# Token shift of a norm's input by a transfer, a new order of the groups, and a rebuilt cross-attention stage

## The chip, the core and the metric

The kernel runs on one core of one Trainium2 chip. The metric is the device time of one execution in microseconds (us), median of the runs. The engines are named as in the profile: PE (TensorE matmul) and PEld (its weight loads), DVE (VectorE), ACT (ScalarE), POOL (GpSimd) and SP (SyncE, which here only issues transfers). All data are float32.

## What is computed

x has 32 batches of 128 tokens with 128 features. First comes a cross-attention with 16 query heads of 8 features and 4 key/value heads, then six layers, each of a local attention (16 heads of 64, windows of 32 tokens that also see the window before) and a gated feed-forward part:

```
x = x + xattn(layernorm(x), ctx, ctx, deltas, mask, Wq, Wk, Wv, Wo, tw)
  # scores = q k^T / sqrt(8) + tw * log1p(|ct_i - ct_j|) + (1 - mask) * -1e9;  ct = cumsum(deltas)
z = layernorm(x)
for i in range(6):
    z = attn_layer(shift_tokens(z), Wqkv[i], q_scale[i], k_scale[i], Wo[i]) + z
    z = ffn_layer(shift_tokens(z), ln_g[i], ln_b[i], W1[i], b1[i], W2[i], b2[i]) + z
return x + z
# shift_tokens: features 64 to 127 come from the token before (zero for token 0), 0 to 63 stay
# attn_layer: q, k divided by their norms, scaled, rotated; softmax over 64 keys; @ Wo
# ffn_layer: layernorm of its input, @ W1 + b1, a * gelu(gate), @ W2 + b2
```

## The kernel before

Tokens lie on the 128 partitions. z_sb holds z of all batches ([128, 32 x 128]), x1_sb the sum after the cross-attention. There is one program for each engine, written out by hand. Engines meet only through semaphores: `count(per_unit, unit, j)` is the value a semaphore has after step j of a unit, `wait` waits for it. Each engine takes its instructions in order, so a wait holds back all that stands behind it on that engine.

**First stage** (`xslots` / `xslot`, lines 252 to 259, 398, 502, 729, 1019). 35 slots; slot n works on batch A = n, Bt = n - 1, C = n - 2 and D = n - 3. For A: PE transposes ctx and the normed x (lines 1051, 1052), and `ones @ td` (line 1053) gives the cumulated deltas and the mask on all rows; DVE makes mbr, dif and dabs (779 to 783) from these, ACT the logarithm (530) and DVE the bias (801); PE projects q, k and v (1078 to 1080), ACT writes qT (534), DVE kblk (813) and vaug (825). For Bt: four score products of 512 columns on a group of 32 rows each (1030), DVE adds the bias (742) and takes maxima (752), POOL subtracts them (409), ACT takes the exponential (545). For C: 16 transposes of 128 x 128 (1071), ACT copies (523), and P times v (1094), copied by ACT (539). For D: four transposes (1042), division by the row sums (760, 770), a transpose (1060), the product with Wo, called y (1086), and on DVE x1cur = y + x (793), its statistics, a copy to x1_sb (806) and the norm into z_sb (829). `rows` (713) makes on DVE the normed x and both halves of td for the batch after A.

**Second stage** (`slots` / `slot`, lines 237 to 244, 418, 549, 834, 1103). A unit is one batch in one layer: 192 units, one new unit in each slot, some 199 slots. In slot n the engines work on a = n (q, k, v), m = n - 1 (inverse norms, `root`), b = n - 2 (transposes, scores, softmax), c = n - 3 (P times v, `attend`), d = n - 4 (attention's output `attn_out`, second shift and norm, gate) and f = n - 5 (`ffn_out`). The order within a slot is the list of calls at the end of each `slot` function (lines 973 to 994 on DVE, 1279 to 1297 on PE, 653 to 674 on ACT, 476 to 488 on POOL).

Around the second shift: `attn_out` (1225; 16 matmuls, line 1233) writes y to bank 7; DVE's `z_mid` (891) adds z: zm. PE's `shift_tokens` (1237) multiplies the first half of zm by the identity (1242) and the second by a shift matrix (1243) into bank 6. DVE takes statistics from there (`norm_stats` 898, `norm_aggr` 905, `norm_var` 911), POOL the power -1/2 (450), DVE applies them (`norm_apply` 918), PE transposes (1258), ACT scales (620), and the gate and a products follow (1267, 1275). POOL's `residual` (459) adds b2 to the unshifted zm for `z_out` (882) in the next slot.

The q and k products (`proj_qk(j)`, line 1123) use banks 0 and 1 by turns: each waits until `rotary` (852, 855; d_rot) and `square` (563) have read what was there before; `proj_v` (1133) waits for the last two rotaries.

**SP** issues all transfers in one queue, in order. The second stage's own are `shift_v(u)`: six transfers of 64 rows of 2 KB from vt to vs, within SBUF, after ACT has copied v and after PE has done `attend` of unit u - 2. In all there are 1,308 transfers: 1,152 of shift_v; in each layer 17 (wqkv in two pieces, rot, wo, gb 2, b1c 6, w1, w2 3, b2r); and 54 at the start and the end (constants 1, dm 2, x 4, Wq, Wk, Wv, Wo and the time weight 5, q and k scales 2, ctx 32, out 8). gb and b1c are columns of 4-byte rows, FCH cuts 341 features into 128, 128 and 85, so two of the six b1c transfers and one of the three w2 transfers have 85 rows, the others 128. Wk and Wv have 128 rows of 128 bytes, the time weight 128 rows of 4 bytes. At a change of layer SP waits in order for the last use of each weight (`load_qk` 278, `load_v`, `load_o`, `load_ffn` 297, which waits for p_y2, that is `ffn_out` of the layer's last unit).

## Time and profile before

| | |
|---|---|
| median of 3 runs | 3447.68 us (3443.36 to 3448.49) |
| the profiled execution | 3448.77 us, its span 3446.8 us, mean granted PE clock 0.976 |
| busy: PE / PEld | 3301.8 us (96%) / 2378.3 us (69%) |
| busy: DVE / ACT / POOL | 2931.5 (85%) / 2735.7 (79%) / 2502.3 us (73%) |
| the chain that ended last | PE 76%, POOL 9%, issue 7%, DVE 4%, DMA 1% |

### The profile page before, as it was taken

Reading aid. Unit: us, or ns where it says so; the run is one execution under the profiler, and the core shown is the slowest. Engines: PE = TensorE matmul, PEld = TensorE weight load, DVE = VectorE, ACT = ScalarE, POOL = GpSimd, SP = SyncE. Lnnn points to the kernel's source line nnn. Section 1 sums busy time; section 2 is a strip of 40 time slices with the busy share of each in tenths; the row PEclk is TensorE's granted clock in tenths of the full one; section 3 lists DMA queues with packets and bytes.
Section 4 is the critical chain, followed back from the end, with each engine's and each line's share of the span. In section 5 each row is a group of like instructions: output and inputs, shape, how many; then the busy total and the mean of one; then the engine's idle time right before and its main releaser. Section 6 shows DMA issues by size and latency. Waiting matters only on the chain.

```text
span 3446.8 us, 169053 instructions
## 1 busy us (share of the span) xinstructions
PE 3301.8 (96%) x65316; PEld 2378.3 (69%) x65316; DVE 2931.5 (85%) x6259; ACT 2735.7 (79%) x5169; POOL 2502.3 (73%) x2671
## 2 busy tenths in 40 slices
PE   5888789999999999999999999999999999999997
PEld 3444357777777777777777777777777777777775
DVE  6888788888888888888888888888888888888885
ACT  3445588888888888888888888888888888888886
POOL 3333377777778777777778777777778777777774
PEclk9778899999999999999999999999999999999998
DMA  2000021212221211222122211212221112212122
GB/s 75 5 6 5 2 55 49 55 46 55 65 68 46 54 51 49 81 53 55 46 55 62 71 50 50 55 46 75 59 55 47 53 52 68 67 46 55 46 55 54
DMA packets 125539, 175.91 MB, mean 51 GB/s; under 512 B 26742, under 2 KB 49332, under 8 KB 124724
## 3 DMA queue, kind: packets, MB, share of 16 engines
q1 hardware_dynamic: 125492, 175.28, 18.9%
q8 instruction: 30, 0.49, 0.1%
q14 instruction: 17, 0.14, 0.0%
HBM read 21.32 MB, written 2.10 MB: 7 GB/s over the span
## 4 chain that ended last, share of the span: by engine, by line
PE 76%; POOL 9%; issue 7%; DVE 4%; DMA 1%; SPq 1%; ACT 1%; POOLq 0%; DVEq 0%; ACTq 0%
PE bank L1123 16%; PE bank L1233 9%; PE bank L1141 9%; PE bank L1133 8%; PE bank L1204 7%; PE bank L1188 6%; POOL qk L435 4%; POOL qk L444 4%; PE bank L1267 3%; PE bank L1221 3%; PE bank L1275 3%; PE bank L1030 2%; PE bank L1071 2%; PE bank L1242 2%; PE bank L1180 2%
## 5 line engine op out<-in xcount | busy, mean ns | idle before, releaser
L435 POOL TENSOR_TENSOR qk<-ta,tb 128x512 f32<-128x512 f32 x768 | 982.8, 1280 | 11.6 <-DVE tb L855 11.6
L1123 PE MATMUL bank<-wqkv,zsT 128*128 128x512 f32 x1536 | 806.4, 607 | 6.1 <-DVE tb L855 2.4
L444 POOL TENSOR_TENSOR qk<-qk,rn 128x512 f32<-128x512 f32 x768 | 796.0, 1049 | 0.0
L563 ACT ACTIVATE sq<-bank 128x512 f32<-128x512 f32 x768 | 461.0, 600 | 322.9 <-PE bank L1123 313.5
L473 POOL TENSOR_TENSOR P<-P,rowsum 128x512 f32<-128x512 f32 x384 | 401.4, 1046 | 374.7 <-DVE rowsum L971 374.7
L852 DVE TENSOR_TENSOR ta<-bank,rot 128x512 f32<-128x512 f32 x768 | 525.8, 685 | 25.4 <-ACT sq L563 10.0
L855 DVE TENSOR_TENSOR tb<-bank,rot 128x512 f32<-128x512 f32 x768 | 521.2, 679 | 0.0
L956 DVE TENSOR_REDUCE bank<-sq 128x32 f32<-128x2048 f32 x192 | 437.8, 2280 | 0.3
L1133 PE MATMUL bank<-wqkv,zsT 128*128 128x512 f32 x768 | 412.3, 619 | 5.0 <-DVE tb L855 5.0
L1233 PE MATMUL bank<-wo,oT 128*128 128x128 f32 x3072 | 393.9, 281 | 1.4 <-ACT oT L589 1.4
L1233 PEld LDWEIGHTS bank<-wo,oT 128*128 128x128 f32 x3072 | 357.4, 191 | 14.6 <-ACT oT L589 1.8
L1141 PEld LDWEIGHTS bank<-cst,qk 64*128 64x128 f32 x6144 | 222.1, 139 | 173.2 <-issue 150.4
L1123 PEld LDWEIGHTS bank<-wqkv,zsT 128*128 128x128 f32 x1536 | 257.1, 198 | 105.1 <-issue 96.5
L1204 PE MATMUL bank<-PT,vs 64*64 64x32 f32 (+1 forms) x18432 | 307.9, 220 | 1.1 <-issue 0.7
L1204 PEld LDWEIGHTS bank<-PT,vs 64*64 64x64 f32 x18432 | 286.5, 135 | 31.7 <-issue 31.7
L450 POOL TENSOR_TENSOR rstd<-ve,half_neg 128x1 f32<-128x1 f32 x192 | 105.7, 550 | 264.4 <-DVE ve L911 264.4
L1188 PEld LDWEIGHTS bank<-kT,qT 64*32 64x32 f32 x24576 | 277.4, 105 | 15.6 <-issue 5.4
L1188 PE MATMUL bank<-kT,qT 64*32 64x64 f32 x24576 | 281.0, 225 | 4.7 <-issue 4.7
L891 DVE TENSOR_TENSOR zm<-bank,z_sb 128x128 f32<-128x128 f32 x192 | 55.9, 291 | 265.1 <-PE bank L1233 265.1
L409 POOL TENSOR_TENSOR qk<-qk,xmax 128x512 f32<-128x512 f32 x128 | 130.0, 1047 | 205.0 <-DVE xmax L752 205.0
L1141 PE MATMUL bank<-cst,qk 64*128 64x64 f32 x6144 | 274.4, 229 | 3.7 <-issue 1.9
L573 ACT ACTIVATE qT<-bank 128x512 f32<-128x512 f32 x384 | 229.1, 597 | 47.8 <-PE bank L1141 47.7
(132 smaller groups left out, 6528.8 us busy)
## 6 DMA issues: line engine op xcount, KB each, us to landing
vs<-vt SPq DMA_DIRECT2D x1152, 128.0 KB, 2.4
wqkv<-L_ffn_Wqkv SPq DMA_DIRECT2D x6, 1024.0 KB, 5.1
wqkv<-L_ffn_Wqkv SPq DMA_DIRECT2D x6, 512.0 KB, 3.8
wo<-L_ffn_Wo SPq DMA_DIRECT2D x6, 512.0 KB, 3.7
z_sb<-x SPq DMA_DIRECT2D x4, 512.0 KB, 6.7
ctxb<-ctx SPq DMA_DIRECT2D x32, 64.0 KB, 1.8
out<-x_sb SPq DMA_DIRECT2D x8, 256.0 KB, 3.5
w<-L_ffn_W SPq DMA_DIRECT2D x6, 341.0 KB, 3.1
```

The source lines that it names most:

```text
L435: g.tensor_tensor(o, i0, i1, ALU.add).then_inc(s["g_add"], 1)
L444: g.tensor_tensor(q3, q3, r3, ALU.mult).then_inc(s["g_qk"], 1)
L563: a_.activation(sq[:, 512 * j:512 * j + 512], bank[j % 2][:, :], ACT.Square)\
L852: v_.tensor_tensor(ta[:, c].rearrange("p (h d) -> p h d", d=DH), bank[j % 2][:, :].rearrange("p (h d) -> p h d", d=DH), rot[:, o:o + 64].u ...
L855: v_.tensor_tensor(tb[:, c].rearrange("p (h c d) -> p h c d", c=2, d=32)[:, :, ::-1, :], bank[j % 2][:, :].rearrange("p (h c d) -> p h c d ...
L956: v_.tensor_reduce(sm, sq[:, :].rearrange("p (h d) -> p h d", d=DH), AX.X, ALU.add)\
L1123: t_.matmul(bank[j % 2][:, :], zsT[:, k % 2, :], wqkv[:, 512 * j:512 * j + 512], start=True, stop=True).then_inc(s["p_qk"], 1)
L1133: t_.matmul(bank[r][:, :], zsT[:, k % 2, :], wv[:, :, r, :], start=True, stop=True)\
L1141: ins = t_.transpose(bank[4 + t][:, 64 * p:64 * p + 64], src[tok, 128 * p:128 * p + 128], ident[tok, tok])
L1188: ins = t_.matmul(SC[e][32 * w:32 * w + 32, 64 * p:64 * p + 64], qT2[dr, p, 32 * w:32 * w + 32], kT2[dr, p, k0:k0 + 64], start=False, stop ...
L1204: ins = t_.matmul(bank[4 + r][64 * e:64 * e + 64, 128 * i + q0:128 * i + q0 + nq], vs[kr, pc, w, hc:hc + 64], PT[kr, 4 * e + i, q0:q0 + nq ...
L1233: ins = t_.matmul(bank[7][:, 384:512], oT[:, p, :], wo[:, 2 * (p % 4) + p // 4, :], start=p == 0, stop=p == PAIRS - 1)
```

## The change

1. **Second shift.** `shift_tokens` on PE goes. zm gets three parts of 64 columns: `z_mid` writes parts 0 and 2, and SP sends part 2 of rows 0 to 126 to part 1 of rows 1 to 127 (`shift_z`); row 0 of part 1 is zeroed once. DVE's statistics and `norm_apply` read parts 0 and 1 from SBUF, after waiting for the transfer (l_s0, l_s1). The other reader, `residual`, takes parts 0 and 2.
2. **Order of the second stage's calls**, on all four engines. `attend` now waits itself for vs.
3. **SP's queue**: `shift_z(u)` stands ahead of `shift_v(u + 3)`, and among the loads at a change of layer.
4. **Root.** The rotary constants are multiplied by 2^8, the logarithm's input and the constant -0.5 by 2^16.
5. **First stage.** td, mbr and dif go: dcur (two columns, copied by POOL) is the stationary operand against tri and ident, ACT takes the absolute value with -ct as bias, and the bias is added from PSUM. The normed x moves from DVE to ACT (`center`, with nmr0 = -mean * rstd), the copy to x1_sb too. P is transposed in 32 pieces of 64 rows. The orders of all four engines change.

```diff
-        zm = sb("zm", [128, 2, E])
+        zm = sb("zm", [128, 2, 3, E // 2])
@@ SP
+            def shift_z(u, par):
+
+                wait(sp, "d_zm", count(1, u, 1))
+                sp.dma_start(zm[1:128, par, 1, :], zm[0:127, par, 2, :]).then_inc(s[f"l_s{par}"], 16)
...
                     for k in range(2):
+                        shift_z(i * 2 + (start + k), k)
                         shift_v(i * 2 + (start + 3 + k), (3 + k) % 2)
+                shift_z(end - 6, 0)
                 shift_v(end - 3, 1)
+                shift_z(end - 5, 1)
                 if layer + 1 < DEPTH:
                     load_qk(layer + 1)
                 shift_v(end - 2, 0)
                 if layer + 1 < DEPTH:
                     load_v(layer + 1)
+                shift_z(end - 4, 0)
                 shift_v(end - 1, 1)
+                shift_z(end - 3, 1)
                 if layer + 1 < DEPTH:
                     shift_v(end, 0)
+                shift_z(end - 2, 0)
+                if layer + 1 < DEPTH:
                     shift_v(end + 1, 1)
                     load_o(layer + 1)
+                shift_z(end - 1, 1)
+                if layer + 1 < DEPTH:
                     shift_v(end + 2, 0)
                     load_ffn(layer + 1)
@@ DVE, second stage
-                        v_.tensor_tensor(zm[:, pd, :], bank[7][:, 384:512], z_sb[:, cols(d)], ALU.add)\
+                        v_.tensor_tensor(zm[:, pd, 0:3:2, :], bank[7][:, 384:512].rearrange("p (c e) -> p c e", c=2),
+                                         z_sb[:, cols(d)].rearrange("p (c e) -> p c e", c=2), ALU.add)\
...
-                        wait(dve, "p_zsh", count(1, d, 1))
-                        v_.bn_stats(stats[:, 0:6], bank[6][:, 0:128]).then_inc(s["d_bn"], 1)
+                        wait(dve, f"l_s{pd}", 16 * (d // 2) + 16 if isinstance(d, int) else (d >> 1) * 16 + 16)
+                        v_.bn_stats(stats[:, 0:6], zm[:, pd, 0:2, :].rearrange("p c e -> p (c e)"))\
+                            .then_inc(s["d_bn"], 1)
@@ PE, first stage
-                    t_.matmul(bank[6][:, 256:512], ones[:, :], td[:, pA, :], start=True, stop=True)\
-                        .then_inc(s["x_A1"], 1)
+                    t_.matmul(bank[6][:, 256:384], dcur[:, pA, 0:1].to_broadcast([128, S]), tri, start=True, stop=True)
+                    t_.matmul(bank[6][:, 384:512], dcur[:, pA, 1:2].to_broadcast([128, S]), ident,
+                              start=True, stop=True).then_inc(s["x_A1"], 1)
```

The orders of the second stage, after (before, they are as printed in the functions above):

```
PE:   proj_qk(0) transpose_qk(0) attn_out proj_qk(1) transpose_qk(1) transpose_z ffn_out proj_qk(2)
      transpose_P scores attend transpose_zn proj_qk(3) proj_v(0) ffn_gate ffn_a proj_v(1)
DVE:  z_mid root(0) rotary(0) root(1) root(2) root(3) norm_stats norm_aggr norm_var z_out rotary(1)
      norm_apply maximum(0) rotary(2) maximum(1) subtract(0) rotary(3) subtract(1) sum_squares gated
      sum_rows invert
ACT:  copy_T(0) copy_T(1) square(0) log_sum square(1) inverse_root copy_T(2) copy_T(3) copy_z
      copy_PT(0) copy_PT(1) square(2) [table] copy_o(0) copy_zn square(3) copy_v(0) copy_o(1) gelu
      [table] exponent copy_v(1)
POOL: norm_rstd add(0) add(1) next_input normalize(0) residual normalize(1) normalize(2) normalize(3)
      add(2) add(3) weigh(0) weigh(1)
```

The orders of the first stage, after:

```
PE:   xscores(0) xscores(1) transpose_P(0) [D: O transposed] xscores(2) [A: ctx, xn, deltas] xscores(3)
      transpose_P(1) [D: attn transposed] [A: q, k, v] [D: y] [C: P times v]
DVE:  add_bias(0) add_bias(1) [D: 1/sums] maximum(0) [D: attn] add_bias(2) add_bias(3) maximum(1)
      [D: x1cur] [A: kblk] [D: statistics, variance] [A: bias, vaug] [D: norm into z_sb]
ACT:  copy_P(0) [A: abs, cxT] copy_P(1) [D: attnT] center(A + 1) [A: qT] exponent(0) [D: x1_sb]
      [A: logarithm] [C: copy of O] exponent(1)
POOL: subtract(0,0) subtract(0,1) subtract(1,0) [D: power] subtract(1,1) deltas_of(A + 1)
```

## Rows read from the trace of the kernel before

**Rows 1.** Busy time by stretch: start:end, length, engines, granted clock, DMA share, GB/s.

```profile
100.00:200.00 100.00, 81.27 (x416) 47.80 (x415) 83.29 (x219) 48.73 (x93) 37.56 (x41) 0.81 0.02 6
...
2000.00:2500.00 500.00, 498.90 (x10735) 368.12 (x10734) 436.47 (x904) 424.75 (x807) 394.06 (x421) 1.00 0.21 56
```

**Rows 2.** Busy time in one slot of the second stage (columns as in rows 1).

```profile
1602.69:1618.13 15.44, 15.44 (x335) 11.38 (x332) 13.44 (x28) 13.14 (x25) 12.20 (x13) 1.00 0.19 51
```

**Rows 3.** Timeline of PE, one slot of the second stage: start, length, what.

```profile
1602.69 2.05 PE L1233 MATMUL bank<-wo,oT 128*128 128x128 f32 x16
...
1606.17 0.43 PE L1242 MATMUL bank<-zm,cst 128*128 128x64 f32 x2
...
1606.67 1.10 PE L1123 MATMUL bank<-wqkv,zsT 128*128 128x512 f32 x2
...
1618.13 2.05 PE L1233 MATMUL bank<-wo,oT 128*128 128x128 f32 x16
```

**Rows 4.** Timeline of DVE in the same slot; in brackets the idle time before.

```profile
1604.97 0.29 DVE L891 TENSOR_TENSOR zm<-bank,z_sb 128x128 f32<-128x128 f32 x1 [1.67 <-PE bank L1233]
...
1606.87 0.30 DVE L898 BATCH_NORM_STATS2 stats<-bank 128x6 f32<-128x128 f32 x1 [0.17 <-PE bank L1243]
...
1619.00 0.29 DVE L882 TENSOR_TENSOR z_sb<-bank,zmb 128x128 f32 x1 [0.56 <-issue]
...
1620.41 0.29 DVE L891 TENSOR_TENSOR zm<-bank,z_sb 128x128 f32<-128x128 f32 x1 [1.02 <-PE bank L1233]
```

**Rows 5.** Transfers: the page's part 6, then line 285 by itself.

```profile
vs<-vt SPq DMA_DIRECT2D x1152, 128.0 KB, 2.4
...
ctxb<-ctx SPq DMA_DIRECT2D x32, 64.0 KB, 1.8
...
L285 SPq DMA_DIRECT2D rot<-rot_all x6: 484/496/553, 18.5 to 2884.6; - x6
...
DMA to landing us min/median/max: 2.1/3.2/3.3
```

**Rows 6.** The page, part 2: packets of all transfers by size.

```profile
DMA packets 125539, 175.91 MB, mean 51 GB/s; under 512 B 26742, under 2 KB 49332, under 8 KB 124724
```

**Rows 7.** DMA of 953 to 960 us (GB/s in 40 slices), then of 100 to 300 us.

```profile
GB/s 211 129 0 0 0 0 0 0 79 193 170 301 316 295 345 342 342 339 199 67 6 0 0 0 0 0 0 0 0 0 0 0 0 0 0 0 0 0 0 0
...
q1 hardware_dynamic: 2448, 1.12, 1.9%
```

**Rows 8.** First stage: line 1030 in all, then two of its slots on PE.

```profile
L1030 PE MATMUL bank<-kblk,qT x256: 587/692/1218, 27.3 to 399.5; 32*128 32x512 f32 x128
...
216.74 1.23 PE L1030 MATMUL bank<-kblk,qT 32*128 32x512 f32 x4 [1.13 <-DVE kblk L813]
...
227.60 2.19 PE L1030 MATMUL bank<-kblk,qT 32*128 32x512 f32 x4 [2.84 <-DVE kblk L813]
```

**Rows 9.** Timeline of DVE at the end of the first of those slots.

```profile
224.20 0.28 DVE L793 TENSOR_TENSOR x1cur<-bank,z_sb 128x128 f32<-128x128 f32 x1
...
224.73 0.97 DVE L801 SCALAR_TENSOR_TENSOR bias<-lnt,xtwc,mbr 128x128 f32<-128x128 f32 x1
225.62 1.06 DVE L806 COPY x_sb<-x1cur 128x128 f32 x1
...
226.69 0.65 DVE L813 TENSOR_TENSOR kblk<-bank,cst 128x512 f32<-128x512 f32 x1
```

**Rows 10.** Busy time by stretch around those slots (columns as in rows 1).

```profile
216.70:224.76 8.06, 7.67 (x49) 4.52 (x49) 7.64 (x22) 4.66 (x10) 2.79 (x4) 1.00 0.03 8
224.76:227.60 2.84, 0.00 (x1) 0.01 (x1) 2.84 (x8) 2.51 (x3) 1.96 (x3) 0.97 0.00 0
227.60:238.80 11.20, 11.20 (x41) 6.97 (x42) 7.22 (x19) 3.36 (x9) 3.24 (x4) 0.55 0.02 6
```

**Rows 11.** The chain of waits at one change of layer: start, length, what.

```profile
897.21 5.21 DMA wqkv<-L_ffn_Wqkv
...
972.82 3.28 DMA b2r<-L_ffn_b
```

More of the change, by code:

```diff
@@ L40 @@
 NORM_MIN2 = 1e-24
+LN_UP = 2.0 ** 16
 MASKED = -(2.0 ** 120)
@@ L398, in xslot @@
             def xslot(n, k):
+                A1, A1_on = part(n, -1, B)
                 Bt, B_on = part(n, 1, B)
@@ L499, in _, with center @@
             act.wait_ge(s["u_ct"], 1)
-            a_.activation(ctT[:, :], bank[6][:, 64:96], ACT.Copy).then_inc(s["u_ctc"], 1)
+            a_.activation(nct[:, :], bank[6][:, 64:96], ACT.Copy, scale=-1.0).then_inc(s["u_ctc"], 1)
+            def center(A, pA):
+                wait(act, "x_A1", count(1, A - 2, 1, B))
+                if isinstance(A, int) and A <= 4:
+                    act.wait_ge(s["u_nmr"], 1 if A < 4 else 2)
+                a_.activation(xn[:, pA, :], z_sb[:, bass.ds(A * E, E)], ACT.Identity, scale=rstd0[:, bass.ds(A, 1)],
+                              bias=nmr0[:, bass.ds(A, 1)]).then_inc(s["x_xn"], 1)
+            act.wait_ge(s["l_x"], 64)
+            center(0, 0)
             def xslot(n, k):
+                A1, A1_on = part(n, -1, B)
                 A, A_on = part(n, 0, B)
@@ L517, in xslot @@
                     a_.activation(attnT[:, :], bank[7][:, 0:128], ACT.Copy).then_inc(s["x_aTc"], 1)
[L518 to L525 removed]
+                if A1_on:
+                    center(A1, (k + 1) % 2)
                 if A_on:
[L528 to L530 removed]
                     wait(act, "x_A2", count(1, A, 1, B))
@@ L534, in xslot @@
                     a_.activation(qT[:, pA, :], bank[6][:, 0:128], ACT.Copy, scale=XSCALE).then_inc(s["x_q"], 1)
+                exponent(0)
+                if D_on:
+                    wait(act, "x_x1", count(1, D, 1, B))
+                    a_.activation(x1_sb[:, bass.ds(D * E, E)], x1cur[:, :], ACT.Copy).then_inc(s["x_store"], 1)
+                if A_on:
+                    wait(act, "x_dabs", count(1, A, 1, B))
+                    wait(act, "x_bias", count(1, A - 1, 1, B))
+                    a_.activation(lnt[:, :], dabs[:, :], ACT.Ln, bias=1.0).then_inc(s["x_ln"], 1)
                 if C_on:
@@ L539, in xslot @@
                     a_.activation(XO, bank[7][:, :], ACT.Copy).then_inc(s["x_Oc"], 1)
-                if B_on:
-                    for j in range(2):
-                        wait(act, "x_sub", count(4, Bt, 2 * j + 2, B))
-                        pr = XP[:, pB, 1024 * j:1024 * j + 1024]
-                        a_.activation(pr, pr, ACT.Exp).then_inc(s["x_exp"], 1)
+                exponent(1)
             xslots(act, xslot)
@@ L1043, in xslot @@
                     ins.then_inc(s["x_OT"], 1)
+                xscores(2)
                 if A_on:
@@ L1284, in slot @@
                 transpose_qk(1)
-                shift_tokens()
+                transpose_z()
+                ffn_out()
                 proj_qk(2)
-                transpose_z()
                 transpose_P()
                 scores()
+                attend()
                 transpose_zn()
                 proj_qk(3)
-                values_here()
                 proj_v(0)
```

309 lines of the change are left out of this document (150 added, 159 removed).

## Prediction

> **What bounds the kernel now.** I read the stretches first: they show two different programs. In the second stage, which holds some 3,000 of the 3,446.8 us, PE is busy 498.9 of 500 us at a full granted clock, DVE 436, ACT 425, POOL 394; in the first nothing is full: PE 81 of 100 us at a granted 0.81, DVE 83, ACT 49, POOL 38 [rows 1]. Busy shares over the whole run hide that. Then I read one slot of each. A slot of stage two runs from 1602.69 to 1618.13 on PE, 15.44 us, and PE is busy for all of them [rows 2, 3]: its instruction stream is the bound. DVE waits 1.67 us in it, in the next one 0.56 and 1.02 [rows 4], so some 13.7 us of its slot is work. Only 1.7 us lie between PE's bound and DVE's own loop, and they are what the change spends. Stage one starts its score products at 27.3 us, and the last of them at 399.5, some 4 us into the 32nd slot [rows 8]: 31 slots in 368 us, 11.9 us each. Its loop closes through DVE: PE has nothing to do from 224.76 to 227.60 and then starts behind kblk (line 813) [rows 8, 10].
>
> **Second stage: removed.** The two shift products (lines 1242, 1243) hold PE from 1606.17 to 1606.67, 0.50 us [rows 3]. Nothing hides them, PE being full. ffn_out, attend and transpose_z move, with their work unchanged; the places where PE's stream breaks ahead of a nop or a wait change, about as many gone as new, which I cost at 0 and round up for: 15.44 - 0.50 = 14.94, call it 15.0 us for PE alone. What the moves put later has room: z_out writes a z_sb that is read 32 units on; ffn_out needs a gated result that DVE has by then; copy_o moves forward on ACT. On POOL, residual goes behind three adds and copies, and its reader z_out belongs to the next slot. The new factor in the square root's logarithm rides on operands that are there: 0.
>
> **Second stage: added.** SP waits for zm, sends 127 rows of 64 values one partition down, and DVE's bn_stats waits for the landing. The wait is in the middle of DVE's queue: behind it stand z_out, three rotaries (PE's v projections and ACT's next squares wait for them), the maxima, subtractions, the sums and at last the next zm. So DVE's own loop counts, in three pieces. (a) From bn_stats to the next z_out is 1619.00 - 0.56 - 1606.87 = 11.57 us of work [rows 4]; two small root steps leave this stretch (-0.3), z_out comes into it (+0.2), and statistics, aggregate and variance follow each other with nothing between (+0.2): 11.7 us to the next zm. (b) zm itself 0.29 [rows 4] and SP's start 0.1: 0.4. (c) the transfer, L. Loop = 12.1 + L. Under L the first rotary and the four root steps (2.0 us) run, which is why L isn't added whole. PE hides the loop up to 15.0, so up to L = 2.9.
>
> **L.** No transfer of this shape is in the trace. The 128 KB ones (64 rows of 2 KB) land in 2.4 us, the 64 KB ones from HBM (128 rows of 512 B) in 1.8, the one within SBUF (128 rows of 1 KB) in 2.1 at its shortest [rows 5]. All these use 16 engines. Does 127 rows? The page counts 26,742 packets under 512 B [rows 6]. Data of that size is 938 rows a layer (gb 256, b1c 512 + 170), 5,628, and 384 at the start (xwk, xwv, xtw): 6,012. The rest, 20,730, is completions. 1,308 transfers (1,152 of vs, 102 of the layers, 54 at the start) with 16 each would be 20,928: 198 are missing. 18 transfers have 85 rows (12 of b1c, 6 of w2), and 18 x 11 = 198. So 85 = 5 x 17 rows went over 5 engines, not 16. 127 has no divisor but 1: one engine takes all 127 packets. The Trainium skill's page "DMA: Bandwidth & Descriptors" (section on why a DMA increments its semaphore by 16) says just this, that the largest number up to 16 that divides the slowest dimension is used, and names 127 partitions as one engine; by it the sum is the forecast, without it the first rival.
> Price of a packet on one engine: 342 GB/s over 16 engines with 512-byte rows is 24 ns a packet, and in the first stage 1.9% of 16 x 200 us over 2,448 packets is 25 ns [rows 7]. Half the bytes is 12 to 13 ns if time goes by bytes, 25 if by packets. 127 packets: 1.6 to 3.2 us. The fixed part is 2.1 less 8 packets of 1 KB, 1.75; from the other rows 1.6 to 2.1. L lies between 3.2 and 5.3; a shorter one than 2.1 [rows 5] isn't to be had. I take 3.35, by bytes, since the rows of 512 B go at a rate set by bytes. The loop is then 12.1 + 3.35 = 15.45 to 15.5 us: the 0.50 us that PE gives up comes back as DVE's wait. 187 steady slots x 0.05: +9 us.
> Not late in either case: POOL with 12.20 and ACT with 13.14 us of work a slot [rows 2], whose queues keep their lengths. SP issues one more transfer a slot; shift_z stands ahead of shift_v, whose wait for attend now ends some 3 us earlier in the slot, so that its six transfers are done when the next zm comes. Without that, shift_z would land behind 128 KB transfers on the same engine. The memset of the row 0 and its wait are at the start: 0.
>
> **Changes of layer.** SP's queue is in order. Now a change of layer costs about 1.3 us (stalls behind the 5.21 us wqkv load and the 3.28 us b2r load [rows 11]). New: the q,k load's stall grows by about 1.5, since attend no longer stands between the last q,k product and the next layer; shift_z(end-1) stands behind the 512 KB of wo (about +2); shift_z of the next layer's first unit stands behind load_ffn, which waits for ffn_out, now later in the slot, and then issues four more (about +3); less what DVE's slack takes. I take 4.5 x 5 = +22 us, bounds 0 and 40. The last three slots, whose chain has nothing beside it: 3 x 1.7 = +5.
>
> **First stage.** DVE loses mbr, dif, dabs (0.8 us with waits), the two td rows and xn, and the copy to x1_sb, which took 1.06 us beside POOL's subtraction as line 801 took 0.97 [rows 9]. After y the way to the next scores was 224.20 to 227.60, 3.4 us: x1 0.28, statistics, bias, copy, aggregate, kblk 0.65 [rows 8, 9]. Now kblk follows x1: 0.3 + 0.65 + 0.25 = 1.2. Saved 2.2 of a slot of 10.86 (216.74 to 227.60). ACT takes on center, Abs and the store, 0.3 each beside 5.8 us of its own (49% of 11.9), which lengthens the copies that y waits for by some 0.3. 32 transposes with 64 rows take PE no longer than 16 with 128; xscores(2) and (3), no longer adjacent, lose their overlap, up to +0.6, partly behind DVE. Slot: 10.86 - 2.2 + 0.3 = 8.9 at the full clock. The clock was granted at 0.55 for the 11.2 us after the idle 2.84 us, and stayed full behind idles near 1.1 [rows 8, 10]. The new idle is about 0.3 to 0.6, so I expect it full, and 31 x (11.9 - 8.9) = -93, and +1 for nmr0 ahead of center at the start: -92. Bounds: +20 (low clock throughout, PE then needs 13 us and more a slot) and -110.
>
> **Sum**, against the profiled execution, 3448.8 (span 3446.8; 1.1 above the median of the runs): 3448.8 + 9 + 22 + 5 - 92 = 3393.
>
> **Rivals.**
> *One: the transfer is cheap* (16 engines, or L under 2.9). For it: 2.1 us in rows 5. Against: the 198 missing completions. PE bounds at 15.0: 187 x -0.44 = -82, changes +10, tail +3, stage one -92: 3288. Chance 0.17.
> *Two: the transfer is dearer by packet* and the kernel slower. Place: bn_stats' wait. Price: each 1 ns of a packet is 0.127 us a slot, 24 us in all. It decides from where it eats what stage one gives, 92 - 27 = 65 us: 0.35 us a slot, a loop of 15.8, L = 3.7, 15 ns a packet. At 20 ns, L = 4.3 and the loop is 16.4: 187 x 0.96 + 27 - 92 = +115, 3563; at 25 ns 3680. For it: half as many bytes needn't halve the time. Against: 512-byte rows stream at the byte rate. Chance 0.28.
> *Three: stage one gives nothing*, since the clock stays low or ACT's longer in-order queue (exponent(1) ahead of copy_P(0)) takes the place of DVE's. With the forecast's second stage: 3485. For it: ACT sits between every two steps of PE. Against: ACT was 49% busy. Chance 0.10.
> *Forecast*, 0.45.
>
> **Chances and range.** A measurement of this kernel tells about 0.2% (7 us). Faster: forecast nearly whole 0.43, rival one 0.17, a bit of three: 0.62. Slower: nearly all of rivals two and three: 0.32. Same: 0.06. The range goes from rival one to 20 ns a packet in rival two: 3288 to 3565; the 25 ns end is left out. The forecast's own range is 3340 to 3440.
>
> **What would show it.** Landing of the shift_z line 3.2 to 3.6 us, against 2.1 (rival one) or above 3.7 (two). DVE idle before bn_stats with the DMA as releaser, about 1.3 us a slot; PE no longer without gaps, its v projection waiting for tb. 15.5 us from one zm to the next. In stage one no idle over 1 us on PE, clock 1.00, starts 8.9 us apart. The forecast is wrong if PE stays full in stage two, or if completions of the new line show 16 engines.

## The result and the profile after

The changed kernel takes 3615.31 us (median of 4 runs, 3609.59 to 3618.62) where the kernel before takes 3448.09 beside it: a ratio of 1.0485, with a 95% interval of 1.0465 to 1.0505. It is 167 us slower. The forecast was 3393, the range ended at 3565.

The two stages went opposite ways. The first transposes of the second stage start at 345.88 us instead of 418.69, so the rebuilt first stage gives 72.8 us; the second stage takes 3270.8 us of the span of 3616.7 instead of 3028.1, which is 242.7 more.

Busy time by stretch after the change, with the columns of [rows 1]: one in the first stage, one in the second, and the last is two slots of the second.

```profile
100.00:200.00 100.00, 91.30 (x725) 49.21 (x721) 88.82 (x209) 69.22 (x154) 51.60 (x66) 1.00 0.02 7
2000.00:2500.00 500.00, 468.74 (x9836) 321.98 (x9834) 416.36 (x837) 385.15 (x749) 363.64 (x387) 0.99 0.20 53
1707.41:1740.51 33.10, 31.25 (x662) 21.46 (x660) 27.90 (x56) 25.72 (x50) 24.39 (x27) 1.00 0.19 50
```

In the first stage the granted clock is now 1.00 where it was 0.81 [rows 1]. In the second PE has lost its full stream: 468.7 of 500 us instead of 498.9, and nothing else is full either. A stage in which every engine has idle time has a closed chain with a wait in it. The timeline of DVE shows it, over the same two slots:

```profile
1707.41 0.29 DVE L926 TENSOR_TENSOR zm<-bank,z_sb 128x128 f32<-128x128 f32 x1 [0.58 <-issue]
1711.42 0.29 DVE L934 BATCH_NORM_STATS2 stats<-zm 128x6 f32<-128x128 f32 x1 [1.67 <-DMA zm<-zm]
...
1723.79 0.29 DVE L926 TENSOR_TENSOR zm<-bank,z_sb 128x128 f32<-128x128 f32 x1
...
1727.80 0.29 DVE L934 BATCH_NORM_STATS2 stats<-zm 128x6 f32<-128x128 f32 x1 [1.71 <-DMA zm<-zm]
...
1729.90 0.63 DVE L955 TENSOR_SCALAR zn<-zm,mv,rstd 128x128 f32<-128x128 f32 x1
1730.45 0.68 DVE L962 TENSOR_REDUCE rowmax<-bank 128x8 f32<-128x512 f32 x1
...
1734.64 0.67 DVE L971 TENSOR_TENSOR P<-bank,rowmax 128x512 f32<-128x512 f32 x1
1735.45 2.29 DVE L993 TENSOR_REDUCE bank<-sq 128x32 f32<-128x2048 f32 x1
...
1740.51 0.29 DVE L926 TENSOR_TENSOR zm<-bank,z_sb 128x128 f32<-128x128 f32 x1 [0.58 <-issue]
```

From one zm to the next lie 16.38 and 16.72 us by turns. Before there were 15.44 and 15.50, 15.47 as a mean, with waits for PE of 1.02 and 1.67 us in front of zm [rows 4]. Those waits are gone: DVE now has no slack. In their place stand 1.7 us before the statistics, put down to the transfer, and 0.58 us at every second zm, put down to issue: that is the edge of the loop, whose pass holds two slots. SyncE starts the transfer 0.32 us behind the start of zm:

```profile
1707.73 0.64 SPq L329 DMA_DIRECT2D zm<-zm  x1
```

so it has landed, and the statistics start, 3.69 us later. The page puts the whole of it in one line of its part 5, and the packets in part 2, which answers to [rows 6]:

```profile
DMA packets 150118, 182.19 MB, mean 50 GB/s; under 512 B 51318, under 2 KB 73908, under 8 KB 149300
...
L934 DVE BATCH_NORM_STATS2 stats<-zm 128x6 f32<-128x128 f32 x192 | 56.6, 295 | 358.4 <-DMA zm<-zm 358.4
```

There are 24,579 packets more; 192 x (127 + 1) are 24,576: 127 rows and one completion a transfer. One engine took them all.

On PE, in the second of these slots, the stream breaks where the prediction looked for it, ahead of the v projection:

```profile
1728.90 1.60 PE L1251 MATMUL bank<-PT,vs 64*64 64x64 f32 x96
1730.58 0.33 PE L1291 MATMUL bank<-cst,zn 128*128 128x128 f32 x1
...
1732.38 1.12 PE L1179 MATMUL bank<-wqkv,zsT 128*128 128x512 f32 x2 [0.59 <-DVE tb L891]
```

Attend (line 1251) ends just as zn is there (1729.90 + 0.63) for its transpose at line 1291. The run with attend in its old place, further down, shows what this cover is worth.

The first stage: score products in all, then the starts of two slots.

```profile
L1071 PE MATMUL bank<-kblk,qT x256: 587/687/1218, 31.0 to 324.8; 32*128 32x512 f32 x128
...
203.87 1.23 PE L1071 MATMUL bank<-kblk,qT 32*128 32x512 f32 x4 [0.28 <-DVE kblk L839]
...
213.01 1.24 PE L1071 MATMUL bank<-kblk,qT 32*128 32x512 f32 x4 [0.29 <-DVE kblk L839]
```

A slot is 9.14 us here, and 9.4 as a mean (31.0 to some 3 us before 324.8, 31 slots), against 11.9. The idle ahead of the scores fell from 1.13 and 2.84 us [rows 8] to 0.3.

At a change of layer SyncE issues the feed-forward's twelve loads before it comes to the transfer of the next batch. First SyncE, then DVE:

```profile
2004.78 0.34 SPq L303 DMA_DIRECT2D gb<-L_ffn_ln_g  x1
...
2010.47 0.66 SPq L329 DMA_DIRECT2D zm<-zm  x1
```

```profile
2006.71 0.29 DVE L926 TENSOR_TENSOR zm<-bank,z_sb 128x128 f32<-128x128 f32 x1 [0.58 <-issue]
...
2015.10 0.29 DVE L934 BATCH_NORM_STATS2 stats<-zm 128x6 f32<-128x128 f32 x1 [6.04 <-DMA zm<-zm]
...
2028.15 0.29 DVE L926 TENSOR_TENSOR zm<-bank,z_sb 128x128 f32<-128x128 f32 x1 [0.27 <-PE bank L1275]
```

A transfer ready for issue at 2007.0 goes out at 2010.5, and the slot takes 21.4 us.

### The profile page after: what moved, and what is told of

Read it like the earlier page. It is cut to its first block, busy times and chain, and to the rows that moved or that the text cites. A ratio compares the mean times of both kernels' runs of the same rounds, so it can differ in the third digit from the quotient of the medians.

```text
span 3616.7 us, 168541 instructions
## 1 busy us (share of the span) xinstructions
PE 3312.3 (92%) x65124; PEld 2232.7 (62%) x65124; DVE 2955.2 (82%) x6037; ACT 2693.5 (74%) x5265; POOL 2504.6 (69%) x2704
## 4 chain that ended last, share of the span: by engine, by line
DVE 39%; issue 25%; DMA 20%; PE 11%; DVEq 3%; ACT 1%; SPq 1%; POOL 0%; ACTq 0%; POOLq 0%
DMA zm<-zm 19%; DVE tb L891 7%; DVE P L971 6%; DVE bank L1000 5%; DVE hT L983 4%; DVE ta L888 4%; DVE rowmax L962 4%; PE bank L1071 3%; DVE zn L955 3%; DVE stats L934 2%; DVE zm L926 1%; DVEq L218 1%; PE bank L1169 1%; PE bank L1088 1%; DVE mv L942 1%
## 5 line engine op out<-in xcount | busy, mean ns | idle before, releaser
L469 POOL TENSOR_TENSOR qk<-ta,tb 128x512 f32<-128x512 f32 x768 | 964.2, 1278 | 14.0 <-DVE tb L891 14.0
L1169 PE MATMUL bank<-wqkv,zsT 128*128 128x512 f32 x1536 | 817.8, 615 | 50.5 <-DVE tb L891 40.4
L478 POOL TENSOR_TENSOR qk<-qk,rn 128x512 f32<-128x512 f32 x768 | 786.0, 1046 | 0.0
L509 POOL TENSOR_TENSOR P<-P,rowsum 128x512 f32<-128x512 f32 x384 | 392.8, 1044 | 267.2 <-DVE rowsum L1008 267.2
L1179 PE MATMUL bank<-wqkv,zsT 128*128 128x512 f32 x768 | 435.3, 649 | 109.4 <-DVE tb L891 109.4
L648 ACT ACTIVATE vt<-bank 128x512 f32<-128x512 f32 x384 | 225.8, 588 | 228.7 <-PE bank L1179 228.7
L1169 PEld LDWEIGHTS bank<-wqkv,zsT 128*128 128x128 f32 x1536 | 247.8, 191 | 183.5 <-issue 95.0
L934 DVE BATCH_NORM_STATS2 stats<-zm 128x6 f32<-128x128 f32 x192 | 56.6, 295 | 358.4 <-DMA zm<-zm 358.4
L664 ACT ACTIVATE PT<-bank 128x512 f32<-128x512 f32 x384 | 208.4, 595 | 188.2 <-PE bank L1187 188.2
L1179 PEld LDWEIGHTS bank<-wqkv,zsT 128*128 128x128 f32 x768 | 116.6, 190 | 301.8 <-DVE tb L891 292.6
```

What stands on the lines that cost most here:

```text
L469: g.tensor_tensor(o, i0, i1, ALU.add).then_inc(s["g_add"], 1)
L478: g.tensor_tensor(q3, q3, r3, ALU.mult).then_inc(s["g_qk"], 1)
L509: g.tensor_tensor(pr, pr, rowsum[:, 8 * j:8 * j + 8].unsqueeze(2).to_broadcast([128, 8, DH]), ALU.mult).then_inc(s["g_P"], 1)
L1169: t_.matmul(bank[j % 2][:, :], zsT[:, k % 2, :], wqkv[:, 512 * j:512 * j + 512], start=True, stop=True).then_inc(s["p_qk"], 1)
L1179: t_.matmul(bank[r][:, :], zsT[:, k % 2, :], wv[:, :, r, :], start=True, stop=True)\
```

## The experiments

Times are medians; "against before" is the ratio to the kernel before, run beside it, with its 95% interval.

### The two halves

Each half of the change by itself: the first stage new and the second old, then the reverse. The diffs are those of the change, cut at the border of the stages.

> The first stage of the changed kernel with the second stage, SP's queue and the constants of the kernel before. If the stages are independent, the second stage keeps its 3028 us and the first gives its 73 us (it ends at 345.9 instead of 418.7 us): 3375 us. If the new first stage owes part of its gain to work that it leaves to the second, the time is above 3390.

Measured 3374.35 us, against before 0.9787 (0.9771 to 0.9804).

> The first stage of the kernel before with the changed second stage. If the stages are independent: 3615 + 73 = 3688 us, slots of 16.4 and 16.7 us by turns. If the slow slots come from something that the new first stage sets up, below 3650.

Measured 3681.67 us, 1.0682 (1.0665 to 1.0700). The halves are -73 and +234 us, together +161 against a measured +167. They can be judged apart: the first stage alone is a gain, and the loss is the second's.

### The transfer

The 127 rows cut in two, and then no transfer at all.

```diff
-sp.dma_start(zm[1:128, par, 1, :], zm[0:127, par, 2, :])...
+sp.dma_start(zm[1:113, par, 1, :], zm[0:112, par, 2, :])...
+sp.dma_start(zm[113:128, par, 1, :], zm[112:127, par, 2, :])...
```

> The changed kernel, with the transfer of 127 rows cut into one of 112 and one of 15 rows. Theory (127 rows go over one engine, 112 over 16 and 15 over 15): SP issues twice, 0.64 us each, and the second lands some 1.7 us after its issue starts, so bn_stats starts 3.0 us after zm's end instead of 3.7; the wait shrinks from 1.7 to about 1.0 us and the time to 3615 - 0.65 x 187 = 3493 us; completions rise from 1 to 31 a unit. Rival (the price is the fixed latency of any transfer, the number of engines doesn't matter): the second issue comes on top, the wait grows to 2.3 us, 3730 us.

Measured 3416.78 us, 0.9907 (0.9891 to 0.9924): two transfers in the place of one take 199 us off. The page's part 6 now has a landing for each:

```profile
zm<-zm SPq DMA_DIRECT2D x192, 28.0 KB, 1.8
...
zm<-zm SPq DMA_DIRECT2D x192, 3.8 KB, 1.9
```

DVE's wait falls from 1.7 to 0.55 us a slot, though SyncE issues one after the other and the second starts 0.6 us late. The time is below what even the theory gave: that had left a wait of 1.0 us.

```diff
-wait(sp, "d_zm", ...)
-sp.dma_start(zm[1:128, par, 1, :], zm[0:127, par, 2, :])...
...
-wait(dve, f"l_s{pd}", ...)
+wait(dve, "d_zm", ...)
```

> The changed kernel without the transfer: the shifted half that the norm reads is left at zero, and statistics wait for zm alone. Theory (the transfer's wait is what makes DVE's loop the bound): the slot loses the wait of 1.7 us, DVE's loop is 14.85, PE's 15.0 binds, and 3615 - 1.5 x 187 - 30 at the changes of layer = 3305 us. Rival (the new order is what costs, since PE waits for rotaries that now stand further back in DVE's queue): the slot stays above 15.5 and the time above 3400 us.

Measured 3390.96 us, 0.9842 (0.9823 to 0.9861). That is 224 us under the change and 26 under the two transfers, so the transfer's wait is nearly the whole loss. But it isn't the theory's time: without any transfer a slot still takes 15.28 and 15.59 us by turns, and the kernel is no faster than with the old second stage and its two shift products.

```profile
1706.53 0.29 DVE L925 TENSOR_TENSOR zm<-bank,z_sb 128x128 f32<-128x128 f32 x1 [0.59 <-issue]
...
1721.81 0.29 DVE L925 TENSOR_TENSOR zm<-bank,z_sb 128x128 f32<-128x128 f32 x1
...
1737.40 0.29 DVE L925 TENSOR_TENSOR zm<-bank,z_sb 128x128 f32<-128x128 f32 x1 [0.59 <-issue]
```

So the 0.5 us that PE gave up isn't had with this order and a pass of two slots; the combined kernel below gets it in part. What holds the slot is DVE's loop together with waits for its neighbours: 0.59 us at every second zm, some 0.26 before the first maximum (for PE's scores) and 0.2 to 0.3 before a rotary (for ACT's squares). With 112 and 15 rows the slots are the same, 15.27 and 15.59 us, so the steady slots no longer pay for the transfer there. The 26 us between the two kernels arise at the changes of layer, where the two transfers still stand behind the loads: from zm to zm, the five slots around each change take 5 to 7 us longer than usual with them, and no longer without.

```diff
-sp.dma_start(zm[1:128, par, 1, :], ...)
+sp.dma_start(zm[1:64, par, 1, :], zm[0:63, par, 2, :])...
+sp.dma_start(zm[64:128, par, 1, :], zm[63:127, par, 2, :])...
```

> The changed kernel with the transfer of 127 rows cut in one of 63 rows and one of 64. Theory (127 rows of 256 bytes go through one DMA engine one after the other, and each costs about 15 ns, (3.65 - 1.8)/127; the 64 rows are spread over 16 engines): the 63 rows land 2.6 to 2.8 us behind their issue, the 64 rows 1.7 to 1.9 us behind theirs, and the kernel takes 3405 to 3450 us, as with 112 and 15 rows. Rival (a transfer on one engine has a fixed price, whatever its rows): the 63 rows land 3.4 us or more behind their issue, 3560 us or more.

Measured 3424.76 us, 0.9938 (0.9918 to 0.9958). The time is the theory's, but the run was not the test it was meant to be: its page counts 154,726 packets, 192 x 24 more than the change. 64 rows have 16 completions, so the 63 rows have 9, and went over 9 engines, not one. The largest divisor up to 16 explains all the counts here: 127 rows 1, 63 rows 9, 112 and 15 rows 16 and 15 (155,878 packets, 192 x 30 more than the change). So 66 and 61 rows:

```diff
+sp.dma_start(zm[1:67, par, 1, :], zm[0:66, par, 2, :])...
+sp.dma_start(zm[67:128, par, 1, :], zm[66:127, par, 2, :])...
```

> The changed kernel with the transfer cut in 66 rows (11 engines by the divisor rule) and, behind it, 61 rows (one engine): packets 150,118 + 192 x 11 = 152,230. Theory (a row costs (3.7 - 1.85)/120 = 15.4 ns on its engine, so 61 rows land 1.75 + 61 x 0.0154 = 2.7 us behind their issue, which starts 0.5 to 0.8 us behind that of the first): the statistics start 3.5 to 3.8 us behind the start of zm, against 4.01 in the changed kernel and 2.89 with 112 and 15 rows, and the slot is shorter by as much, 0.2 to 0.5 us: 3520 to 3580 us. Rival (one engine is a fixed price of 3.7 us): the statistics start 4.5 us or more behind zm, and the kernel takes 3690 us or more.

The packets first, then the second transfer's issue and the statistics:

```profile
DMA packets 152230, 182.20 MB, mean 51 GB/s; under 512 B 53430, under 2 KB 76020, under 8 KB 151412
```

```profile
1709.07 0.68 SPq L330 DMA_DIRECT2D zm<-zm  x1
```

```profile
1707.84 0.29 DVE L927 TENSOR_TENSOR zm<-bank,z_sb 128x128 f32<-128x128 f32 x1
1711.71 0.29 DVE L935 BATCH_NORM_STATS2 stats<-zm 128x6 f32<-128x128 f32 x1 [1.57 <-DMA zm<-zm]
```

The packets are 152,230, to the packet what the rule gives. 61 rows on one engine take 2.64 us, 127 take 3.69: 16 ns a row, and no fixed price of one engine. Measured 3581.05 us, 1.0387 (1.0364 to 1.0410), 1 us above the expected band: zm to statistics is 3.87 us, not 3.5 to 3.8, as the first issue takes 0.87 us of SyncE and the second starts 0.91 us behind it, not 0.5 to 0.8.

### What is queued around the wait

The statistics further down DVE's list, and POOL's power behind its first two additions:

```diff
 root(3)
-norm_stats()
-norm_aggr()
-norm_var()
-z_out()
 rotary(1)
-norm_apply()
+z_out()
+norm_stats()
+norm_aggr()
+norm_var()
 maximum(0)
+norm_apply()
```

> The changed kernel with one move: on VectorE the statistics of the second norm, their aggregate and the variance stand behind the second pair of rotary products and the addition of the feed-forward, the first row maximum stands ahead of the norm's application, and POOL's power stands behind its first two additions. The transfer is as it was. Theory (what is lost is the 1.7 us that VectorE waits in each slot for the transfer, and 1.24 us of rotary products and the addition can cover it): the slot falls from 16.55 us towards the 15.44 of the kernel without a transfer, so 3400 to 3470 us. Rival (the transfer holds up something else, or the order is the bound): above 3550 us.

Measured 3505.02 us, 1.0172 (1.0140 to 1.0204): 110 us better than the change, short of the 145 to 215 expected. The wait for the transfer falls to 0.2 us, but 0.46 us appear before the first maximum, which waits for PE's scores, and the norm's application, now right behind the power on POOL, takes 895 ns as a mean and not 534. Covering a wait moved others into DVE's chain.

```diff
-slots(dve, slot)
+slots(dve, slot, 4)
```

> The changed kernel, with four slots in each pass of VectorE's loop alone (46 passes); the loops of the other engines keep their two slots, so that TensorE's instructions are fetched as before. Theory (in the changed kernel VectorE's list is the bound, so its 0.58 us of idle at each loop edge is paid whole): 46 edges less at 0.58 us, 27 us less, 3580 to 3600 us. Rival (TensorE or ScalarE takes the place of the edge at once): 3608 us or more.

Measured 3586.75 us, 1.0407 (1.0381 to 1.0432): 29 us for 46 edges, 0.62 us each. The edge is paid whole.

The same for all engines:

```diff
-LOOP0, UNROLL = 6, 2
+LOOP0, UNROLL = 6, 4
```

> The changed kernel with four slots in each pass of the loop of all four engines instead of two (46 passes instead of 92); nothing else is changed. Theory (VectorE's 0.58 us of idle at each loop edge stands in its closed chain, so a pass costs it whole): 46 edges less at 0.3 to 0.6 us, 3587 to 3602 us. Rival (the edge is covered, as the 50 us of it in the kernel before were): 3612 to 3618 us.

Measured 3954.29 us, 1.1461 (1.1419 to 1.1503), against 3587 to 3602. The instruction queues of the page, of the change and then of this run:

```profile
q8 instruction: 31, 0.51, 0.1%
```

```profile
q8 instruction: 576, 9.44, 1.0%
...
L1251 PE MATMUL bank<-PT,vs 64*64 64x32 f32 (+1 forms) x18432 | 353.5, 223 | 217.7 <-issue 217.7
```

576 fetches in the place of 31: instructions are fetched again in each pass, and PE stands idle, put down to issue, in the middle of attend (217.7 us) and of the scores (76.0 us). The rest of the 339 us isn't taken apart; the granted clock is 0.95 from 1000 to 2000 us, where the change has 1.00. The DVE loop of four alone didn't do that (31 and 19 on the two queues, as in the change). That PE's pass is the one that is too long is read from whose waits are put down to issue; ACT and POOL had four slots too.

```diff
 for o, src in ((0, lng), (1, lnb)):
     sp.dma_start(gb[:, o:o + 1], ...)
+if layer:
+    shift_z(B * layer, 0)
 for h in range(2):
```

> The changed kernel with one move on SyncE: at each of the five changes of layer, the transfer of the token shift of the new layer's first batch is issued behind the two loads of the norm's scale and bias, ahead of the other ten loads of the feed-forward's tensors, instead of behind all twelve. Theory (VectorE idles 6.04 us there for a transfer that SyncE issues 3.8 us late, so the changes of layer cost some 4.3 us more than a slot's own wait, in the place of the 22 us for all that the prediction gave them): 17 to 24 us less, 3591 to 3600 us. Rival (behind that wait TensorE waits for the feed-forward's tensors, which are now later): 3608 us or more.

Measured 3598.66 us, 1.0442 (1.0420 to 1.0464): 17 us less, at the edge of the band. The slot of 21.4 us now takes 16.4.

### Order and transfer apart

The new order with the shift back on PE, and the old order with the transfer. As bank 6 then holds the shifted tokens, ffn_out and z_out keep their early places in the first of them.

```diff
 proj_qk(0)
+ffn_out()
 transpose_qk(0)
...
 transpose_qk(1)
+shift_tokens()
 transpose_z()
-ffn_out()
...
 z_mid()
+z_out()
 root(0)
```

> The rebuilt first stage and the new order of the second stage's instructions, but the token shift is again the two TensorE products into bank 6 (ahead of the transpose of z), and there is no transfer. To keep bank 6 for one engine at a time, the product of the feed-forward's second half and the addition that takes it stay where they were before the change (behind the first q/k projection, and behind the second norm's input on VectorE); all the rest has the new order. Theory (the transfer and the wait for it are the loss, the new order costs little): the slot is that of the kernel without a transfer, 15.3 to 15.6 us, plus up to 0.35 us of the two products: 3375 to 3440 us. Rival (the new order alone costs the loss, whatever shifts the tokens): above 3500 us.

Measured 3981.57 us, 1.1544 (1.1504 to 1.1584): far off. PE, idle in the bracket:

```profile
1734.81 0.93 PE L1263 MATMUL bank<-w,hT 128*128 128x128 f32 x6 [1.88 <-DVE hT L983]
```

ffn_out early in PE's list waits for gated(), which the new order puts behind DVE's 2.3 us sum of squares. With that one swap undone:

```diff
-sum_squares()
 gated()
+sum_squares()
```

> The kernel of the new order with the shift on TensorE, with one move on VectorE: the gated product stands ahead of the sum of squares again, as before the change. In the run without this move TensorE idles 352 us (1.9 us in each slot) for the gated product, since the product that reads it had to stay early in TensorE's list. Theory (that place alone made the miss, and the new order itself is harmless): the slot is 15.0 us of TensorE, 0.35 to 0.5 of the shift and up to 0.4 of waits for the first rotary products, 15.4 to 15.9: 3365 to 3460 us. Rival (attend and the scores ahead of the last q/k projection cost it): 3600 us or more.

Measured 3503.55 us, 1.0151 (1.0124 to 1.0178). The wait is gone and with it 478 us, more than the 352 us of the wait itself. The other part goes with the clock: with the wait it was granted at 0.96 from 1000 to 2000 us and slots of 17.9 and 19.5 us stand side by side, without it at 1.00. So that place made most of the miss; but at 44 us above the expected band this is between theory and rival. The slots are 16.0 us, with DVE waiting 0.60 for the scores, 0.25 for squares, 0.44 for PE's attn_out and 0.35 put down to issue. PE is busy 981 of 1000 us there. With PE shifting, this new order (ffn_out, z_out and gated in their early places) is worse than the old one by 129 us.

The reverse, old order and transfer:

```diff
-shift_tokens()
...
-wait(dve, "p_zsh", ...)
+wait(dve, f"l_s{pd}", ...)
```

> The rebuilt first stage and the old order of the second stage's instructions on all engines; the two TensorE products of the token shift are taken out and the transfer of 127 rows stands in their place, with SyncE's list of the change. Theory (the wait for the transfer is in VectorE's loop in any order): landing 3.65 us behind the issue, with 12.1 us of VectorE's loop behind it, gives slots of 15.75 to 16.2 us against 15.47, 190 times: 3425 to 3515 us. Rival one (the old order hides the transfer, the new order is the culprit): 3374 us or less. Rival two (the transfer costs the same 1.1 us of a slot in any order): 3580 us or more.

Measured 3869.58 us, 1.1235 (1.1198 to 1.1272), which is the second rival's side and beyond: the transfer is dearer in the old order than in the new one, 17.8 us a slot. PE:

```profile
1738.63 0.41 PE L1226 MATMUL bank<-maskb,selb 64*32 64x512 bf16 x8 [1.22 <-issue]
...
1741.01 0.33 PE L1295 MATMUL bank<-cst,zn 128*128 128x128 f32 x1 [0.71 <-DVE zn L955]
```

The scores start behind the last root step, which the old order queues behind the statistics on DVE. With the two root steps ahead of the wait:

```diff
-norm_stats()
 root(2)
-norm_aggr()
 root(3)
+norm_stats()
+norm_aggr()
 norm_var()
```

> The kernel of the old order with the transfer, with one move on VectorE: the last two steps of the root stand ahead of the statistics and so ahead of the wait for the transfer. In the run without this move TensorE idles 1.22 us ahead of the scores, which wait for the last root step, and 0.71 us ahead of the transpose of zn, of slots of 17.82 us. Theory (what is queued behind the wait on VectorE is what makes the old order dearer): 1.22 us of a slot less, 190 times, 230 us less, 3600 to 3700 us. Rival (POOL's list, whose first entry waits for the variance, is the chain, so nothing changes): 3820 us or more.

Measured 3990.02 us, 1.1574 (1.1550 to 1.1599): neither theory nor rival, but 120 us slower. The wait of the scores is gone, and the one for zn takes all of it:

```profile
L1295 PE MATMUL bank<-cst,zn 128*128 128x128 f32 x192 | 64.3, 335 | 417.4 <-DVE zn L955 417.4
```

That is 2.2 us a slot where it was 139.5 us in all. So zn was the chain. What makes it slower than before is the clock: granted 0.95 from 1500 to 1800 us, where the run with the two shorter waits had 0.98. Slots of 17.8 us are there as before, and between them now slots of 19.4 to 19.5. The roots' place doesn't explain why the new order is cheaper, then. Attend's place was left, taken back in the changed kernel on PE, with the two copies of its result behind the exponential on ACT:

```diff
 scores()
-attend()
 transpose_zn()
 ...
 ffn_a()
+attend()
 proj_v(1)
...
-copy_o(0)
 copy_zn()
 ...
-copy_o(1)
 ...
 exponent()
+copy_o(0)
+copy_o(1)
```

> The changed kernel with attend back in its old place on TensorE (behind the feed-forward's products, ahead of the last v projection) and the two copies of its result behind the exponential on ScalarE; VectorE, POOL and SyncE are those of the change. Theory (VectorE's late zn, 2.8 us behind the start of the statistics, is covered on TensorE by attend's 1.6 us, which ends 0.1 us ahead of it; without that cover TensorE idles 1.5 us ahead of the transpose of zn, and attn_out, which sets the next zm, comes later by that, less the 0.3 to 1 us that VectorE's zm has in hand): a slot longer by 0.4 to 1.3 us, 3690 to 3860 us, and 1.2 to 1.6 us of TensorE's idle time a slot put down to zn. Rival (attend's place is indifferent, the old order lost its time elsewhere): 3640 us or less.

Measured 3961.39 us, 1.1489 (1.1470 to 1.1508). PE's wait for zn over the run, and the granted clock behind it in two slots that follow each other:

```profile
L1291 PE MATMUL bank<-cst,zn 128*128 128x128 f32 x192 | 64.1, 334 | 337.2 <-DVE zn L955 337.2
```

```profile
1704.18:1709.95 5.77, 5.17 (x17) 3.41 (x17) 5.64 (x9) 2.63 (x7) 5.77 (x8) 0.70 0.00 0
1723.19:1728.85 5.66, 5.07 (x113) 3.61 (x113) 5.53 (x9) 3.63 (x7) 5.66 (x7) 1.00 0.00 0
```

1.76 us a slot, a little above the 1.2 to 1.6 expected. Most slots take 17.8 us, 1.3 more than in the change and the theory's upper end; those in which the clock falls take 19.1 to 19.4, and they carry the time past 3860. So attend's place, with that of its copies, softens the transfer in the new order by some 350 us: 1.3 us in each of 187 slots are some 245 of them, and the rest goes with the clock.

### All that helped, together

112 and 15 rows, DVE's loop of four, the shift ahead of the loads, whose diffs stand above, and on POOL:

```diff
+pool.wait_ge(s["u_dmc"], 2)
+g.tensor_copy(dcur[:, 0, :].unsqueeze(2), dmT[:, :, 0:1])...
 pool.wait_ge(s["l_cst"], 16)
 pool.wait_ge(s["l_qks"], 32)
...
-if isinstance(n, int) and n == 0:
-    pool.wait_ge(s["u_dmc"], 2)
-    deltas_of(0, 0)
```

> All that helped, together: rebuilt first stage, new order, transfer in 112 and 15 rows, VectorE's loop of four slots, the token shift ahead of the loads at the changes of layer, and the copy of the first batch's deltas ahead of the rotary table on POOL. Theory (the parts add up: 3417 us with 112 and 15 rows, less 24 at the changes of layer, 4 at the start, and 0 to 27 of loop edges, as far as the slot of 15.44 us is above TensorE's 15.0): 3362 to 3392 us. Rival (what is left of VectorE's wait is replaced by ScalarE's squares or TensorE's scores, so that no edge counts): 3385 to 3400 us; either is set against the 3374 us of the rebuilt first stage alone.

Measured 3363.42 us, 0.9763 (0.9739 to 0.9787), as the parts add up. Starts of zm:

```profile
1539.92 0.29 DVE L928 TENSOR_TENSOR zm<-bank,z_sb 128x128 f32<-128x128 f32 x1 [0.57 <-issue]
1555.22 0.29 DVE L928 TENSOR_TENSOR zm<-bank,z_sb 128x128 f32<-128x128 f32 x1
1570.23 0.29 DVE L928 TENSOR_TENSOR zm<-bank,z_sb 128x128 f32<-128x128 f32 x1
1585.24 0.29 DVE L928 TENSOR_TENSOR zm<-bank,z_sb 128x128 f32<-128x128 f32 x1
```

The last two slots, without an edge, take 15.01 us each, with PE full: the prediction's 15.0 for PE alone is seen here. The slot behind an edge takes 15.30, the one with it 15.6. So with fewer edges the new order does reach PE's bound in two slots of four. Now with a DVE pass of eight slots, `slots(dve, slot, 8)`:

> The combined kernel with eight slots in each pass of VectorE's loop instead of four (23 passes). Theory (each edge of 0.58 us is paid whole, since slots without one take 15.0 to 15.3 us and those with one 15.6): 23 edges less, 13 us less, 3344 to 3356 us. Rival (TensorE, which is busy for all but 0.4 of 62 us there, takes their place): 3360 us or more.

Measured 3440.69 us, 0.9981 (0.9967 to 0.9996), 77 us slower than with four. Most slots within a pass do take 15.0, but the edge is another one:

```profile
q14 instruction: 154, 1.25, 0.1%
```

```profile
1579.78 0.29 DVE L928 TENSOR_TENSOR zm<-bank,z_sb 128x128 f32<-128x128 f32 x1 [3.15 <-issue]
```

DVE's instructions, too, are fetched again. PE waits 2.54 us for that zm, and its clock is granted at 0.83 over the 10 us that follow (1580 to 1590 us), so the slot behind the edge is long as well, 15.5 to 17.2 us. The last run is the new first stage with the old second one and the same earlier copy of deltas:

> The rebuilt first stage with the old second stage, and the copy of the first batch's deltas ahead of the rotary table on POOL. Theory (TensorE's first product of the first stage starts 4 us earlier, as that copy waited behind POOL's power): 3366 to 3373 us, 0.3 to 0.8% above the combined kernel with a loop of eight. Rival (the start is bound by the loads, so nothing changes): 3374 us.

Measured 3366.20 us, 0.9773 (0.9742 to 0.9803). PE's first product comes 4.2 us earlier (22.39 for 26.54 us), and the time is 8 us less, within what two medians differ by. Against 0.9763 for the combined kernel that is no difference: the new order of the second stage, with its transfer made cheap, ends where the old order with two products on PE already is.

## Why the prediction was wrong

**The bound, right.** PE at 15.0 us without its shift products is seen in the combined kernel, 15.01. DVE's loop as the thing to count, with the transfer's wait in its middle, was right as a mechanism, and so was the one engine: the packet counts of four cuts agree.

**L, mis-sized.** 3.35 us were taken, from 12.6 ns a row "by bytes"; it is 3.69, and a row costs 16 ns. That is the mechanism of the second rival (half the bytes don't take half the time), and the very value at which it was to decide, 3.7. The Trainium skill names 127 partitions as one engine ("DMA: Bandwidth & Descriptors", the section on why a DMA increments its semaphore by 16), and the counts agree. With SyncE's part, 0.32 and not 0.4, L makes +0.26 us of the slot.

**The loop behind the wait, the step that failed.** Step (a) gave 11.7 us from the statistics to the next zm; the trace has 12.37 and 12.71, 12.54 as a mean, so +0.84 us. The largest piece is 0.29: the step took DVE's 0.56 us of "issue" [rows 4] out as idle, where it is the price of the loop's edge every second slot. It was free before since PE's wait of 1.02 us stood behind it, and it costs 0.58 once DVE is the chain; DVE's loop of four slots got 29 us back. The rest is small gaps between neighbours. The norm's application takes 0.36 and 0.55 us of DVE's time by turns and not 0.32, the sum of squares starts 0.81 us behind the second subtraction where gated started 0.59 behind it, the aggregate has 0.2 us more to wait in every second slot. DVE before the change, for comparison:

```profile
1608.86 0.40 DVE L918 TENSOR_SCALAR zn<-bank,mv,rstd 128x128 f32<-128x128 f32 x1
1609.18 0.68 DVE L852 TENSOR_TENSOR ta<-bank,rot 128x512 f32<-128x512 f32 x1
...
1613.37 0.68 DVE L934 TENSOR_TENSOR P<-bank,rowmax 128x512 f32<-128x512 f32 x1
1613.96 0.85 DVE L946 SCALAR_TENSOR_TENSOR hT<-bank,b1c,gl 128x128 f32<-128x128 f32 x3
```

"Nothing between" was said of the order of the list, and it isn't so in time. Of these pieces only the edge has a run of its own; the gaps are read from the timelines, and what makes them stays open. The loop is 16.55 us where 15.45 stood. Against the old slot, 15.47 as a mean, that is 1.08 us, 187 times: +202 us, where the forecast had +9.

**PE hides the loop up to L = 2.9, wrong for the same reason.** With no transfer at all the slot is 15.4 us. The first rival's time, 3288, was met by no run: with two transfers that land in 1.8 and 1.9 us it is 3417, with the loop of four and the moves at the start and at the changes of layer on top 3363.

**Changes of layer.** +27 us forecast with the tail, some +41 measured (242.7 less 202). The mechanism was right, the next layer's shift behind load_ffn; moving it gave 17 us back by the medians, 25 in the slots around the changes. Those slots hold some 27 of the 41 us; most of the rest lies in the first and last slots of the stage.

**First stage.** -92 forecast, -73 measured. The slot is 9.14 us where 8.9 stood, 9.4 as a mean, which is 15 us of the difference; the start costs 4.2 us and not 1 (PE's first product of the stage at 26.09 us and not 21.85), as the copy of the first deltas, new on POOL, stood behind the rotary table and the power that waits for the norms. The clock stayed full as expected, and DVE is again the loop: kblk follows x1 at once.

**The sum.** 193 us of slots, 14 of changes and 19 of the first stage make 226 us above the forecast of 3393; the profiled execution, 3618.5, is 225 above it. The second rival had the right place, and at 15 ns a packet the right L; but with the same 12.1 for the rest of the loop it gave 15.8 us a slot there, and a kernel that is no slower.

What stays open is why the new order, with ffn_out, z_out and gated in their early places, is 129 us worse than the old one when PE shifts; that kernel has four short waits on DVE, and none was tested by itself.

## What to carry to other kernels

When an engine that had slack becomes the chain, its gaps count: loop edges, small gaps between instructions and waits for a neighbour that the old profile shows as harmless are then paid in full. Measure that engine's loop from one start to the next, and don't take its idle time out unless the change removes what causes it. For a small transfer inside a chip's memory, choose the number of rows for its divisors (112 and 15 rows took 1.8 and 1.9 us where 127 took 3.7), count the completions to see how many engines it had, and measure the halves of a change apart: here the first stage gives its 73 us without the transfer.

## What the hardware showed that was not expected

- A loop edge on DVE is 0.58 us. A pass of four slots still has that, one of eight has 3.15 us and 154 fetches where there were 19. With four slots on all four engines there are 576 fetches for 31, and the kernel is some 340 us slower.
- A longer wait on PE can be worse than two short ones. With 1.22 and 0.71 us in each slot (old order with the transfer) the granted clock was 0.98 in the mean of 300 us. With one long one in most slots it was 0.95: 2.0 us with the roots ahead of the wait, 1.9 us in the new order with the shift on PE, 1.5 to 1.7 us with attend in its old place. Behind PE's wait of 1.67 us for zn the run with attend in its old place shows 0.70 over 5.8 us, so 1.2 GHz for part of it, and behind that of 1.47 us in the next slot 1.00, which is 2.4 GHz. What decides between the two isn't shown. A wait that is moved or merged can thus cost more than its own length.
- One transfer of 127 rows is dearer than two issued one behind the other that carry the same rows: 199 us over the run, though SyncE is kept busy longer (0.55 and 0.86 us of issue against 0.64).
